# A layer stack on one core: another order of the units in each engine's queue, and another bank table

## The reference

```
x = x + attn0(norm(x))          # 16 heads of 8, softmax over 256 keys, no output projection
x = x + relu(norm(x) @ w1) @ w2 # 512 wide
x = x + attn1(norm(x))          # rotary, causal, 16 heads of 8, output projection
y = norm(x)
for l in range(2):              # two layers of local attention
    y = y + local_attention(shift(y) @ wqkv[l]) @ wo[l]   # 8 heads of 64, window 64, q and k l2-normed, rotary
    h = norm(shift(y)) * g + b
    y = y + (a * gelu(gate)) @ w2[l] + b2[l]              # a, gate = split(h @ w1[l] + b1[l])
x = x + y
```

## Time and profile before

| | us |
|---|---|
| median of 3 runs (lowest, highest) | 3128.42 (3126.73, 3133.96) |
| the profiled execution | 3130.85 |
| its span, first to last instruction | 3128.7 |
| PE busy | 2816.9 (90%) |
| DVE busy | 2411.2 (77%) |
| ACT busy | 2147.9 (69%) |
| POOL busy | 1548.2 (49%) |

### The profile page before, as it was taken

How to read it: one execution, slowest core, us unless ns; L and a number is a source line. 1 busy time by engine, 2 the same in 40 slices (tenths; PEclk the granted TensorE clock), 3 DMA queues, 4 the chain that set the end, 5 groups by cost and what they waited for, 6 DMA issues and landing times.

```text
span 3128.7 us, 65895 instructions
## 1 busy us (share of the span) xinstructions
PE 2816.9 (90%) x22656; PEld 1976.8 (63%) x22656; DVE 2411.2 (77%) x6016; ACT 2147.9 (69%) x5956; POOL 1548.2 (49%) x1741
## 2 busy tenths in 40 slices
PE   3678999999999999999999999999999999998875
PEld 1455666666666666666666666666666666666553
DVE  3367888888888888888888888878888888777653
ACT  2356777777777777677777767777776777776653
POOL 1034554555545455554555554545555555545542
PEclk7689999999999999999999999999999999999987
DMA  2000000000000000000000000000000000000000
GB/s 67 3 3 4 5 6 6 5 6 6 6 5 7 6 4 6 6 6 6 5 7 6 5 6 6 6 5 7 6 5 6 6 6 5 6 4 4 4 5 5
DMA packets 41974, 21.76 MB, mean 7 GB/s; under 512 B 21131, under 2 KB 41013, under 8 KB 41653
## 3 DMA queue, kind: packets, MB, share of 16 engines
q1 hardware_dynamic: 41652, 17.55, 2.0%
HBM read 9.17 MB, written 4.19 MB: 4 GB/s over the span
## 4 chain that ended last, share of the span: by engine, by line
PE 43%; DVE 27%; ACT 19%; POOL 5%; issue 4%; DMA 0%; DVEq 0%; POOLq 0%; SPq 0%
DVE negmax L836 10%; ACT rawP L730 6%; ACT P L730 5%; PE bank L1050 5%; PE bank L1143 5%; PE bank L1151 4%; PE bank L1030 4%; PE bank L1096 3%; DVE ss L879 3%; PE bank L1159 3%; POOL rn L633 3%; PE bank L1130 2%; ACT probs L697 2%; PE bank L1085 2%; PE bank L1011 2%
## 5 line engine op out<-in xcount | busy, mean ns | idle before, releaser
L836 DVE TENSOR_REDUCE negmax<-bank 128x2 f32<-128x512 f32 (+1 forms) x896 | 554.4, 679 | 25.7 <-PE bank L1011 25.6
L697 ACT ACTIVATE probs<-bank 128x512 f32<-128x512 f32 (+1 forms) x1024 | 480.9, 568 | 131.8 <-PE bank L1030 129.5
L633 POOL TENSOR_TENSOR rn<-ss,minus_half 128x16 f32<-128x16 f32 x128 | 372.6, 2911 | 172.0 <-DVE ss L894 171.4
L582 POOL TENSOR_TENSOR veps<-moments,eps_tile 128x2 f32<-128x2 f32 x192 | 38.2, 199 | 785.4 <-DVE moments L788 785.4
L1085 PE MATMUL bank<-wqkv_sb,hS 128*128 128x512 f32 x768 | 390.9, 625 | 30.9 <-ACT P L730 12.7
L914 DVE TENSOR_REDUCE negmax<-bank 128x2 f32<-128x384 f32 (+1 forms) x384 | 211.7, 593 | 135.1 <-PE bank L1118 133.4
L600 POOL TENSOR_SCALAR_AFFINE_SELECT probs<-probs 128x256 f32<-128x256 f32 x512 | 225.2, 463 | 166.8 <-ACT probs L697 166.4
L1050 PE MATMUL bank<-probs,V 128*16 128x256 f32 (+1 forms) x4096 | 259.5, 373 | 24.4 <-ACT probs L697 22.2
L1011 PE MATMUL bank<-kT,qT 32*128 32x256 f32 (+1 forms) x2048 | 216.8, 324 | 25.7 <-DVE negmax L836 16.1
L1085 PEld LDWEIGHTS bank<-wqkv_sb,hS 128*128 128x128 f32 x768 | 131.9, 193 | 163.3 <-issue 125.6
L730 ACT ACTIVATE rawP<-bank,negmax 128x128 f32<-128x128 f32 x512 | 179.7, 376 | 79.7 <-DVE negmax L914 79.7
(11 more groups left out here) (138 smaller groups left out, 7299.2 us busy)
## 6 DMA issues: line engine op xcount, KB each, us to landing
xin<-x SPq DMA_DIRECT2D x32, 128.0 KB, 2.1
out<-xout SPq DMA_DIRECT2D x32, 128.0 KB, 1.8
V<-YB SPq DMA_DIRECT2D x64, 63.5 KB
wqkv_sb<-wqkv SPq DMA_DIRECT2D x1, 1536.0 KB
V<-YB SPq DMA_DIRECT2D x64, 0.2 KB
w_sb<-w SPq DMA_DIRECT2D x1, 682.0 KB
w_sb<-w SPq DMA_DIRECT2D x2, 256.0 KB
wo_sb<-wo SPq DMA_DIRECT2D x2, 256.0 KB
```

The lines of the kernel that those rows point to most:

```text
L633: nc.gpsimd.tensor_tensor(rn[:, l, t].rearrange("p m h -> p (m h)"), ss[:, l, t].rearrange("p m h -> p (m h)"), minus_half[:], ALU.pow).th ...
L697: nc.scalar.activation(dst, src, ACT.Exp, scale=SCALE0 if k == ATTN0 else SCALE1)\
L836: nc.vector.reduce_max(negmax[:, k, t, head:head + 4 * many - 3:4], tile(u, e)[:, :].rearrange("p (h k) -> p h k", h=many), AX.X, negate=T ...
```

## The change

Only tables change: the five strings of `FIRST`, `TURNS` and `LAST` (one for each engine), and the three bank strings. Each engine runs the same instructions on the same data as before. `FIRST` has two units more and `LAST` two fewer, and the round is as long as before. The rows of a table tell a reader nothing, so two stand here for all:

```
@@ TURNS, BANKS @@
     "vector": (
-        "0003311111002222202233111202033333333222222222222333321112333331110000031123321110003000113333310002"
+        "0300001113022220220332023333333311122222222222233332211133333311100000231132110001113333330000001222"
 BANKS = (
-    "1567045123064701627304156273504152730412763207165210367213456471320571356015243012704603745126702545"
+    "7612507314607325173726451736245601273261504315043105430712502653471746324507136457103503764201726350"
```

More of the change, by code:

```diff
@@ L77 @@
+        "1100000011100110001101110001001110001000111010002001111111222222000000222222222011111110001001100000"
+        "0111001101122222222210020221100022222212222222200211100011100011222200022020011111122122200000022222"
+        "22222201111211100030011100003331112222223"
     ),
     "scalar": (
[L79 to L80 removed]
@@ L81 @@
-        "1111222222222111222222222222111000000000022200011100000111100002222222222111111100000002210022222211"
-        "110000222002222223003003301111111222223"
+        "0000000000000000000000000000000000000000000000000000000000000000000000001111000000010011110000000000"
+        "1111111111111111000000000001001110000001111000211111112222220000000100222222222111100000000001111111"
+        "1111112222222221222112222221000000000022222200011100000111102222222000222111111221000000022200122211"
+        "11222222222000030000003331111111112222223"
@@ L93 @@
-        "1111111112222222222222222222222222111111110000000000000000000000000000000000011110000022222222222022"
-        "222222222223332233000000000111111111112"
+        "0000000000000000000000000000000000000000001111000000000000000000000000000000000000000010111111111111"
+        "1111111111111111111111100000000000000000000000000000000000222220000012220222222222211111111111111122"
+        "1111111112222222222222222222222222111111110000000000000000000000000000000000011122222222200000221222"
+        "02222222222223333300000000111111111111122"
@@ L132 @@
-        "3333333333333333333333333333333333333333333333333333333333113"
+        "0330110222000121200133321110033333310222222222222002233333332331100033310002222110003333133313223203"
+        "3300221111133130000222222122200222221111033331333111333113233333333111112222222221112221112222222222"
+        "2222111233333333333333313113131222222333332333333311111331322122222212222222211121133333331111333333"
+        "3331111122222222211122213333333332222122122222222111233333333313311311333332222333222333333223222222"
@@ L141 @@
+        "2111333333333333333311113222222232333333223333331111111221222222222222221111233333333333333331111111"
+        "1133311222222222111223333333323222222111222222111333333333331111333332222222333322233332222222222222"
+        "2222333333333333333322222222233333322233333322222222222233333333333333333333333322222222223333333333"
+        "33333333333333333333333333333333333333333333333333330111233"
     ),
     "vector": (
-        "0003311111002222202020233232222233333331112222222332211133333331112311320000030003111110000001223333"
@@ new lines @@
+        "0010033333330113222222213323000022111112222222233331113113331223333322333222221111122333333322222222"
+        "2222233222111331111113333311233211313221122333331333333311332122223222311111122332332222222111131333"
+        "3322223332222222331111111123333333322222222222223333211111123333331123323111333332221233333333322222"
+        "2223222322222223333322223333333222223233323333333222222233332223333332222332333333333333232322222332"
+        "33333333333333333333333333333333333333333333333333333333333"
@@ L156 @@
-        "3333333333333333333333333333333333333333333333333333333333331"
+        "1131133333331311133333311122222222222222222222222111111110000000000000000000000000001112222222222200"
+        "0001233333333333333333333333332222222222233333323223333331111111111111113311333133333333311111122222"
+        "2222222222222222222211111122222211111122222333333333333333333333333322222222222233333323333223311111"
+        "1111111111333111333333333111333111222222222222222222222222222222211111122222222333333333333333333333"
```

95 lines of the change are left out of this document (38 added, 57 removed).

## The result

The changed kernel takes 3094.53 us in the median of four runs (3089.05 to 3097.26), the kernel before 3129.08 beside it: a ratio of 0.9892, interval 0.9876 to 0.9907. That is 34.5 us faster, where 69 were forecast. The profiled execution took 3092.75 us, its span is 3091.0.

What follows compares the result with a forecast made beforehand. PE was taken as the bound nearly everywhere, waiting on a DVE stretch. DVE's -1.64 and PE's -0.9 made -2.54 us a round, 69 us over 27 rounds: 3130.85 to 3062, 3060 as median; range 3023 to 3091.

Steps and rivals of the forecast that it cites:

- The clock: PE's clock drops, 27 us in all before: taken as 0 change, since the wait where it falls stays.
- (a): POOL's L613 goes behind the second L621, so DVE's L894 ends sooner and PE's 0.56 wait ends: -0.6 us a round.
- (b): DVE's L804 on `V` goes behind three `qkv2` rows, which fill the wait for stream 3's 1/sqrt: -0.74 us a round.
- (c): DVE's L804 and L902 meeting POOL's SBUF pieces: 1.7 us in place of 2.2, so -0.5 us a round.
- (d): `shift_rows` moves inside DVE's stretch; its copy L793 with memset adds 0.2 us a round.
- (e): PE's eight L992 with maxima go ahead of the second pair's L1143, hidden in the stretch: -0.9 us a round.
- (f): PE's 0.73 wait for a bank at 1613.73 goes, but 0.5 to 0.8 is expected at `scores2`: 0.
- The ends: PE's idle time at the kernel's start and end: 0 change, with 10 us either way.
- the meetings only move: Rival: DVE still meets POOL's pieces, one or two more than forecast; 3091 to 3112 us, chance 0.22 for 3091 to 3122.
- Another loop: Rival: another circle of waits holds the round, DVE's relief becomes a wait elsewhere; 3122 to 3135 us, chance 0.10.
- The slower case: Rival: POOL's L613 for `down2` waits for ACT's late L657 and delays DVE; 3163 us if 5.5 late, chance 0.14.
- The time of the changed kernel that I had worked out from the page, 3103: Case: POOL's powers (L633) hold up DVE's copy L793, +1.6 us a round, 3103 us; chance 0.04.

Runs made afterwards that it cites:

- experiment 8: On experiment 1's kernel, PE's fourth qkv2 product (L1085) put ahead of the transposition L969 of `V`: 3068.99 us, ratio 0.9838.
- experiment 9: PE's first up2 product moved ahead of L969 on `probs` in the changed kernel, 3082.14 us; moved behind it in the kernel before with (a), 3123.27 us.
- experiment 7: The eight L992 with maxima moved alone on the kernel before, 3174.35 us; the changed kernel with only that move undone, 3169.91 us.
- experiment 4: The kernel before with (a) and with DVE's L804 on `V` behind the three qkv2 rows: 3100.06 us, ratio 0.9919.
- experiment 1: The changed kernel with POOL's 1/sqrt of stream 0 (L582, L585) put back ahead of the first `add2` (L628): 3052.13 us, ratio 0.9771.

## Why the prediction was wrong by half

The forecast was 2.54 us a round of schedule, and 0.80 came. The clock, forecast at 0, gave 14 us; without it only some 21 of the forecast 69 us would have come. By its own steps:

(a) held: L894 0.55, PE's wait gone, 0.50 to 0.6 a round for 0.6.

(b) and (c) are where it failed first. With (d) they were to shorten DVE's queue by 0.74 + 0.5 - 0.2 = 1.04. In this sum 0.9 is the meeting of L902 on `rawB`, which lies behind the stretch, so the stretch itself was to shrink by 1.94; it shrank by 0.35. The wait for stream 3's 1/sqrt did go, and the copy L793 did run in 0.22 us under L633, as the rows said; but with its memset it took 0.39 us of the stretch, not 0.2. The step that failed is the sentence "L902 then runs under the second pair of powers: nothing". L902 did run in 0.68. It was POOL that paid, 0.57 us on L585, and DVE then waited 0.60 for L585. I had asked what a meeting costs DVE and never what it costs POOL. The second error of (c) is in "meets L613 (0.73): +0.3": the two L804 met L613 and L628 one after the other, +1.47. The meeting of L804 on `V` cost 0.14, not 0.5. That closes the sum: 1.94 - 0.60 - 1.17 + 0.36 - 0.19 = 0.34. The +0.9 for L902 on `rawB` did not come (0.68). With the 1/sqrt put back, the same stretch is 1.60 shorter than before.

(e) failed too: 0.9 was forecast and the rest of the period, apart from (a), is 79.74 before and 79.79 after. The step that failed is "PE would have waited at this place for the exponentials and copies of ACT, so the work is hidden". PE has no wait of over 0.15 us from 1589.91 to 1613.73 in the kernel before, and none from 1572.63 to 1590.60 in the changed one. The L992 were moved from one place in full work to another, and they stand on the chain of waits in their new place, 0.94 us together, as they did in the old one, 0.87:

```profile
1573.47 0.50 PE bank L992 x4
...
1574.30 0.44 PE bank L992 x4
```

The picture behind it, "the length of the DVE stretch up to the second pair's `mix2` of stream 2, plus the PE work that stands behind it", is not shown by any run. Experiments 8 and 9 moved 1.0 us of PE work around the end of the short stretch from L828 to the second L879, and the period stayed or grew by 0.15; but this end lies some 35 us ahead of `mix2`, so they say that PE's waits beside DVE's queue are not worth filling, and not where the wide stretch ends. The trace agrees with that much: from 1537.00 to 1579.23 DVE has a single wait of over 0.15 us (0.19, at 1543.56). Only (e) crosses the border that the prediction named, and its two runs (experiment 7) disagree in sign. Which instructions set the 79.8 was not tried and stays open.

(f) as forecast: the wait of 0.73 went, and 0.24, 0.17 and 0.33 came in its place.

The ends: 0.6 and 1.9 us, within the 10 allowed. The clock: the changed kernel spends 31 us of these rounds at 1.2 GHz instead of 68. The prediction put this term at 0 because the wait behind which the clock falls "stays". It didn't: in the kernel before, all 12 drops of these rounds start 0.9 to 3.1 us behind the end of the 0.87 wait ahead of L1030, and this wait is gone. Eight of the nine drops of the changed kernel lie at the new wait of 1.97.

The time lies in the range of the rival "the meetings only move", whose account (one meeting more) is near the truth; but the extra one was on POOL's side. "Another loop" was right in so far as work put into PE's waits gained nothing. The slower case didn't arise: POOL had no wait of over 0.1 us ahead of L613.

## What to carry to other kernels

A wait for another engine and a stretched instruction can be the same thing in two columns: where DVE runs into POOL's SBUF pieces, removing a wait ahead of it may only lengthen the next DVE instruction, as in experiment 4. Price such a stretch by when POOL's queue has a hole, from both engines' side, and look at short pieces like the 1/sqrt here that a DVE instruction needs soon: ahead of POOL's long piece it was worth 1.25 us a round. And test the claim "this engine is the bound" by moving 1 us of its work across the wait before building a sum on it.

## What the runs showed of the hardware

The blocking goes both ways. In the changed kernel L585 takes 1.27 us in all 26 rounds in which L902 starts within 0.04 us of it, and about 1.05 us where it starts 0.2 us into a DVE L902 or L923 of 0.69 us. It is late by 0.57 and 0.35 us, about 0.15 less than what is left of the DVE instruction. Yet L828, also with two SBUF inputs, ran in 0.29 us inside L633. So this power did not block DVE in its middle, and the short one was held up at its start. Which of the two pays is not read from the starts: L585's row begins 0.03 us ahead of L902's and L585 pays, and an L804 on `V` or `probs` whose row begins 0.05 or 0.06 us ahead of L613's or L628's (changed kernel, experiment 1) is the one that ends late. The Trainium skill (SBUF — State Buffer, Who interferes with whom) has the two engines exclude each other for the whole instruction: L902 against L585 agrees, with POOL as the loser, and L793 and L828 inside L633 disagree. The time of the changed kernel that I had worked out from the page, 3103, is nearer to the measurement than mine, but not for its reason, since L793 paid nothing.

Where the granted clock falls, PE has waited. In the changed kernel eight of nine drops start between 0.4 us ahead of the end of the 1.97 us wait and 1.4 us behind it. In the round after the one above, this wait ends at 1627.9, and the clock falls at 1629.3 (windows of 3 us, columns as in the earlier trace rows):

```profile
1624.00:1627.00 3.00, 1.96 (x13) 0.99 (x12) 2.40 (x5) 1.93 (x4) 2.85 (x5) 1.00 0.00 0
1627.00:1630.00 3.00, 2.07 (x9) 1.85 (x10) 3.00 (x6) 0.86 (x2) 3.00 (x3) 0.88 0.00 0
1630.00:1633.00 3.00, 3.00 (x7) 1.73 (x7) 1.91 (x6) 1.30 (x4) 0.25 (x1) 0.55 0.00 0
```

In the third window PE is mostly at 1.2 GHz. A drop costs a round of this kernel 1.0 to 1.8 us. With 1.0 us of the wait filled (experiment 9) all drops but one were gone and the period was the same; with 1.0 us more of waiting in the kernel before with (a), they came in 24 rounds of 26 instead of 10. But the length of one wait doesn't decide it. The wait of 1.97 stands in every round, and 17 of 26 have no drop. In experiment 8 the wait is 0.68 us, and 20 rounds have a drop, some 18 us later, beside waits of 0.15 and 0.30. What decides is not shown here.
